# Masking the local attention's probabilities on GpSimd in place of band products on TensorE, with five probability slots and small weight steps

## The reference

```python
i = jnp.arange(x.shape[1])
diff = i[:, None] - i[None, :]
mask = (diff >= 0) & (diff < WIN)          # local attention, WIN = 32; the global one has diff >= 0 alone
scores = jnp.einsum('bhqd,bhkd->bhqk', q, k) / np.sqrt(HD).astype(np.float32)
scores = jnp.where(mask, scores, jnp.float32(-1e+30))
probs = jax.nn.softmax(scores, axis=-1)    # 16 heads of 8, 4 key heads
...
x = x + global_latent_attn(rmsnorm(x, norm1_w), ...)
x = x + local_gqa_attn(rmsnorm(x, norm2_w), ...)
...
w_q = jnp.clip(jnp.round(W / scale), -1.0, 1.0) * scale     # feed-forward weights, scale = mean |W| of a row
```

## Time and profile before

| what | us |
|---|---|
| median of three runs (lowest, highest) | 529.55 (525.73, 531.33) |
| the profiled execution, its own time | 528.51 |
| its span, from the first to the last instruction | 526.7 |
| PE, DVE, ACT, POOL busy in the span | 435.2, 345.2, 342.2, 197.6 |
| granted TensorE clock, mean of the span (1.00 is 2.4 GHz) | 0.946 |

### The profile page before, as it was taken

One profiled execution on the slowest core, in us unless ns is written; L12 is line 12 of the kernel. 1 busy time (PEld: TensorE's weight loads), 2 busy tenths in 40 slices (PEclk: granted clock), 3 DMA queues, 4 the chain that ended last, 5 costly groups with the idle time before them and its releaser, 6 DMA issues.

```text
span 526.7 us, 15578 instructions
## 1 busy us (share of the span) xinstructions
PE 435.2 (83%) x6044; PEld 226.5 (43%) x6044; DVE 345.2 (66%) x940; ACT 342.2 (65%) x442; POOL 197.6 (38%) x482
## 2 busy tenths in 40 slices
PE   0245899998999999889999998999999998657362
PEld 0122444453464445544564454445545544414231
DVE  2899986755377758858668573655782476664556
ACT  0143689889767889758787983999878975104010
POOL 4458667878334253715311250131330011051101
PEclk9999799999899999999999998999999999679577
DMA  7311421112201010110100011000020000010000
GB/s 198 117 40 42 86 47 42 41 43 46 39 2 41 12 43 3 43 41 12 43 3 1 11 39 5 11 4 2 2 49 7 1 7 7 0 40 13 1 1 10
DMA packets 47528, 15.77 MB, mean 30 GB/s; under 512 B 40536, under 2 KB 46816, under 8 KB 47456
## 3 DMA queue, kind: packets, MB, share of 16 engines
q1 hardware_dynamic: 44032, 12.10, 10.7%
q10 hardware_dynamic: 3424, 2.68, 1.8%
HBM read 4.15 MB, written 1.05 MB: 10 GB/s over the span
## 4 chain that ended last, share of the span: by engine, by line
PE 54%; DVE 20%; POOL 8%; issue 6%; DMA 4%; ACT 4%; SPq 3%; DVEq 0%; POOLq 0%; ACTq 0%
PE osum_g L995 17%; PE scores L966 13%; PE scores L960 4%; PE misc L1094 4%; PE misc L1105 4%; PE misc L995 3%; ACT prob L840 3%; DMA qT<-qe_l 3%; PE misc L1031 2%; DVE early L1419 2%; PE misc L936 1%; DVE early L1221 1%; SPq L686 1%; PE misc L1012 1%; SPq L672 1%
## 5 line engine op out<-in xcount | busy, mean ns | idle before, releaser
L840 ACT ACTIVATE prob<-scores 128x1024 f32<-128x1024 f32 (+3 forms) x352 | 308.0, 930 | 107.0 <-PE scores L966 105.4
L995 PE MATMUL osum_g<-prob,V 128*32 128x256 f32 (+1 forms) x2304 | 150.6, 385 | 2.7 <-POOL prob L782 2.7
L966 PE MATMUL scores<-qT,kT 32*128 32x256 f16 (+2 forms) x1520 | 113.4, 257 | 13.8 <-ACT prob L840 10.4
L995 PEld LDWEIGHTS osum_g<-prob,V 128*32 128x32 f32 x2304 | 63.4, 112 | 56.7 <-issue 30.0
L966 PEld LDWEIGHTS scores<-qT,kT 32*128 32x128 f16 x1520 | 38.9, 92 | 95.8 <-issue 87.4
L782 POOL TENSOR_SCALAR_AFFINE_SELECT prob<-prob 128x512 f32<-128x512 f32 x64 | 42.8, 685 | 79.7 <-ACT prob L840 79.0
L1105 PE MATMUL misc<-t2T,h1p 128*128 128x512 f16 x128 | 34.6, 419 | 13.3 <-DVE h1p L1451 9.7
L1458 DVE TENSOR_TENSOR early<-misc,oh 128x512 f32<-128x512 f32 x32 | 21.9, 684 | 24.0 <-PE misc L1105 22.8
L799 POOL TENSOR_SCALAR frs<-fmv 128x1 f32<-128x1 f32 x16 | 3.1, 196 | 91.0 <-DVE fmv L1474 90.9
L1094 PE MATMUL misc<-early,t1T 128*128 128x256 f16 x256 | 34.0, 293 | 1.5 <-DVEq L1422 1.5
L960 PE MATMUL scores<-band,identb 128*32 128x320 bf16 (+1 forms) x512 | 27.9, 303 | 7.6 <-DMA qT<-qe_l 7.1
(11 more groups left out here) (213 smaller groups left out, 637.9 us busy)
## 6 DMA issues: line engine op xcount, KB each, us to landing
X<-in_L_attn_hidden_dram SPq DMA_DIRECT2D x8, 128.0 KB, 4.8
early<-in_L_ffn_expert_w_dram ACTq DMA_DIRECT2D x1, 1024.0 KB, 7.9
out_dram<-X SPq DMA_DIRECT2D x16, 64.0 KB, 1.5
rope<-in_rope_dram SPq DMA_DIRECT2D x1, 256.0 KB, 3.8
early<-in_L_ffn_shared_w_dram ACTq DMA_DIRECT2D x2, 128.0 KB, 9.0
qT<-qe_l SPq DMA_TRANSPOSE x16, 2.4
kT<-ke_g SPq DMA_TRANSPOSE x8, 2.8
qT<-qe_g SPq DMA_TRANSPOSE x8, 2.7
```

The source lines that it names most:

```text
L840: act.activation(prob[:, n % NP, 2 * half:2 * half + 2, lo:hi], src, ACT.Exp, scale=float(HD) ** -0.5 * QSCALE ** -2).then_inc(exp_done, 1)
L966: ins = pe.matmul(scores[:, 512 * m + c:512 * m + c + w], kT[a][rows, t % kept[a], g, :], query_rows(a, b, g, rows, q, w), start=(a == G a ...
L995: ins = pe.matmul(o[32 * m:32 * m + 32, at + q:at + q + w], V[a][:, t % kept[a], V_AT[g]:V_AT[g] + 32], prob[:, n % NP, m, c:c + w], start ...
```

## The change

For the local units of blocks 0 to 6 PE no longer writes the band; the scores are computed for all of the 320 columns (288 in block 0), the exponential is taken of all of them, and POOL multiplies the probabilities by a table `keep` of ones and zeros, one `tensor_tensor` for each half, in `qkmask`. Block 7 keeps its band (`BANDED = 7`). The table `keep` (128x320 fp32) is one more DMA on ACT's queue, and all waits for that group of DMAs count 15 in place of 14. `prob` has five slots in place of four. `prep` is cut into eight steps and `ternary` into eighteen, and the planner's durations, its delay for DMAs and the table `PULL` are others, so that the order on every engine is another. A step "fill" is in the planner but off (`FILL = 0.0`).

```diff
-NP = 4
+NP = 5
...
-HOP = (0.22, 0.1, 0.08, 0.2, 2.5)
+HOP = (0.22, 0.1, 0.08, 0.2, 2.6)
...
-    "unitg": (749.2, 939.7, 409.5, 154.3, 1050, 121.7, 460.4, 510.3),
+    "unitg": (591.3, 418.6, 393.1, 426.3, 686.7, 411.3, 365.5, 623.9),
...
-        op((DVE, "prep"), 6.8, (DVE, "weights"), earliest=LANDED)
+        for k, t in enumerate((0.35, *[0.95] * 6, 1.8)):
+            op((DVE, "prep", k), t, (DVE, "prep", k - 1) if k else (DVE, "weights"), earliest=LANDED)
...
-        for k, t in enumerate((3.9, 3.9, 2.0, 2.85, 2.85)):
-            op((DVE, "ternary", k), t, (DVE, "prep"), *([(DVE, "ternary", k - 1)] if k else []))
+        for k in range(2 * (NE + 1)):
+            op((DVE, "ternary", k), 1.05 if k <= NE else 0.8, (DVE, "ternary", k - 1) if k else (DVE, "prep", 7))
...
-        op((SP, "qT", a, b), 0.5, (DVE, "split", a, b), *([("Q", a, o, *units_of(a, o)[-1])] if o >= 0 else []))
+        op((SP, "qT", a, b), 1.2 if g else 2.4, (DVE, "split", a, b), *([("Q", a, o, *units_of(a, o)[-1])] if o >= 0 else []))
...
+            kept = diag or not g and b < BANDED
...
-            if diag:
-                op(("M", *u), 1.34, ("E", *u))
+            if kept:
+                op(("M", *u), 1.34 if g else 3.0, ("E", *u))
...
             def qkmask(*u):
                 n = UNIT[u]
+                lo, hi = columns(*u[:2], u[3])
+                if u[0] == L:
+                    pool.wait_ge(wf_in, 16 * 15)
                 for half in range(2):
                     pool.wait_ge(exp_done, 2 * n + half + 1)
+                    if u[0] == L:
+                        d = prob[:, n % NP, 2 * half:2 * half + 2, lo:hi]
+                        k = keep[:, lo:hi].unsqueeze(1).broadcast_to([P, 2, hi - lo])
+                        pool.tensor_tensor(d, d, k, ALU.mult).then_inc(mask_done, 1)
+                        continue
...
+                act.dma_start(keep[:], keep_d).then_inc(wf_in, 16)
...
-                if a == L:
+                banded = a == L and b >= BANDED
+                if banded:
                     lo, hi = columns(a, b, pr)
...
-                                        kT[a][rows, t % kept[a], g, :], query_rows(a, b, g, rows, q, w), start=(a == G and k == 0), stop=True,
+                                        kT[a][rows, t % kept[a], g, :], query_rows(a, b, g, rows, q, w), start=(not banded and k == 0), stop=True,
...
+    keep = (band == 0).astype(np.float32)
```

More of the change, by code:

```diff
@@ L142, in front @@
         op((ACT_E, "xT", a, b), 0.37, (PE, "xT", a, b), *old(DVE, "proj", a, p))
-        op((PE, "proj", a, b), 0.83, (ACT_E, "xT", a, b), *([] if b else [(DVE, "weights") if g else (DVE, "prep")]),
+        op((PE, "proj", a, b), 0.83, (ACT_E, "xT", a, b), *([] if b else [(DVE, "weights") if g else (DVE, "prep", 0)]),
            bank=[((DVE, "proj", a, b), -1.5)])
@@ L149, in front @@
         op((DVE, "split", a, b), 2.99, (POOL, "proj", a, b), *old(SP, "qT", a, p))
-        op((SP, "kT", a, b), 0.5, (POOL, "ksplit", a, b), *([("Q", L, p, KVH - 1, 0)] if b > 1 and not g else []))
+        op((SP, "kT", a, b), 1.2, (POOL, "ksplit", a, b), *([("Q", L, p, KVH - 1, 0)] if b > 1 and not g else []))
         o = b - Q_KEPT[a]
-        op((SP, "qT", a, b), 0.5, (DVE, "split", a, b), *([("Q", a, o, *units_of(a, o)[-1])] if o >= 0 else []))
+        op((SP, "qT", a, b), 1.2 if g else 2.4, (DVE, "split", a, b), *([("Q", a, o, *units_of(a, o)[-1])] if o >= 0 else []))
     def attend(self, a, b):
@@ L198, in feed @@
             op((PE, "fmask", b, i), 0.62, (PE, "fmask", b, 0) if i else (PE, "fohT", b), bank=[((DVE, "fmask", b, i), 0)])
-            op((DVE, "fmask", b, i), 1.32, (PE, "fmask", b, i), (DVE, "fmask", b, 0) if i else (DVE, "fohT", b), (DVE, "ternary", 4))
+            op((DVE, "fmask", b, i), 1.32, (PE, "fmask", b, i), (DVE, "fmask", b, 0) if i else (DVE, "fohT", b), (DVE, "ternary", 2 * NE + 1))
         op((PE, "fw1s", b), 0.95, (DVE, "fohT", b), (PE, "fmask", b, 1), (SP, "wturn", 0), (SP, "wturn", 1),
@@ L373, in make_plan @@
         t, e, k = best
+        late = not queues[G] and not current and not exps
+        while FILL and late and t > free[PE] + FILL / clock.rate + 0.02 and free[PE] > max(half):
+            order[PE].append(("fill", len(units)))
+            free[PE] = clock.run(free[PE], FILL)
         if k[0] == "qk" and e == PE:
@@ L458, in build @@
         band = sb("band", [P, 2 * P + 2 * WIN], BF16)
+        keep = sb("keep", [P, 2 * P + 2 * WIN])
         rank = sb("rank", [P, NE])
@@ L1150, in weights, with prep, limits @@
                 dve.tensor_copy(rwT[:], bank(s, 2)[:, 0:NE]).then_inc(free(s, 2), 1)
[L1152 to L1157 removed]
+            def prep(k):
+                if k == 0:
+                    dve.wait_ge(wf_in, 16 * 15)
+                    dve.tensor_scalar(wqkv[L][:], wraw[L][:], nw[L][:, 0:1], None, ALU.mult).then_inc(wqkv_ready, 1)
+                elif k < 4:
+                    r = slice((k - 1) * (NE + 1) * FT // 3, k * (NE + 1) * FT // 3)
+                    dve.tensor_reduce(s1c[:, r], w1n[:, r, :], AX.X, ALU.add, apply_absolute_value=True)
+                elif k < 7:
+                    r = slice((k - 4) * (NE + 1) // 3, (k - 3) * (NE + 1) // 3)
+                    link(dve.tensor_reduce(s2c[:, r], w2n[:, r, :], AX.X, ALU.add, apply_absolute_value=True))
+                else:
+                    limits()
+            def limits():
                 link(dve.tensor_scalar(s1c[:], s1c[:], 1.0 / P, 1e-5, ALU.mult, ALU.max))
@@ L1217, in ternary @@
                 ter2, low2 = [t.rearrange("p (k d) -> p k d", d=FT * P) for t in (t2, t2b)]
-                rows = sorted({(w, r) for w, r, _ in TURNS[k]})
+                rows = [(1, 2 * k), (1, 2 * k + 1)] if k <= NE else [(2, k - NE - 1)]
                 for w, r in rows:
```

58 lines of the change are left out of this document (26 added, 32 removed).

## The result

The changed kernel takes 558.55 us (median of 4 runs, 558.37 to 560.23) beside 529.64 us of the kernel before (4 runs, 525.73 to 531.33). The ratio is 1.0564, with a 95% interval from 1.0503 to 1.0626. The forecast was 513.0 us, with 498 to 530 as its range: it is wrong in sign.

What follows compares the result with a forecast made beforehand. It took PE to bound the middle stretch (100 to 441 us), DVE the start, and a chain over all engines the end. 528.5 - 20.7 - 3.5 + 5.0 + 3.7 = 513.0 us, range 498 to 530.

Steps and rivals of the forecast that it cites:

- band products removed: PE, local units of blocks 0 to 6: dropping the band products wins 20.7 us, bounds 14.3 and 24.7.
- start, order: Start of the run: earlier key split and q transpose, no wait for `bdiag`; wins 3.5 us, bounds 0 and 9.
- masks on POOL: PE waits for POOL's masks before local products with V: costs 5.0 us, bounds 0 and 29.
- DVE held up: Middle stretch: POOL's multiplications lock DVE out of shared ports; costs 3.7 us, bounds 0 and 22.
- so I let a sixth through: 3.7 us: Middle stretch: of 22 us lost on DVE, a sixth reaches the run time, 3.7 us.
- half of its work as of the kind that is stopped: Middle stretch: DVE busy 0.64, half its work stoppable, so 0.32 of 69 us is lost: 22 us.
- DVE has 124 us free there: Middle stretch, 100 to 441 us: DVE is idle 124 us, a reason for letting little lost time through.
- The sign that it named for this: Sign of the locks: PE waits for DVE's `hm` and `h1p` of over 10 us would show the forecast wrong.
- 220 us free in the middle: Middle stretch: POOL, busy 121 of 341 us, has 220 us free for 81 us of multiplications.
- first rival: Blocks 0 and 1: POOL becomes the bound early and no gain comes before 147 us; 525.4 us, chance 0.14.
- slower rival: Feed-forward and fronts, 100 to 420 us: DVE becomes what PE waits for; 538.8 us at half, chance 0.10.
- second rival: The slower one: DVE, losing 69 us to locks, becomes what PE waits for; 538.8 us at half, chance 0.10.

Runs made afterwards that it cites:

- no mask: Changed kernel with neither band products nor POOL multiplications, so the local mask of blocks 0 to 6 is left out: 515.40 us, 0.9756 against before.
- order with band: Changed kernel's order, tables and five slots, with band products back in blocks 0 to 6 and no POOL multiplication: 531.70 us, 1.0069 against before.
- awaited writes: Changed kernel with two POOL writes of zeros to an unread tile replacing each multiplication, PE waiting for them as for masks: 531.33 us.
- idle writes: Changed kernel with two POOL writes of zeros to an unread tile replacing each multiplication, PE not waiting for them: 535.20 us.
- idle multiplication: Changed kernel with each POOL multiplication done on a tile nobody reads, so PE waits for no mask: 555.27 us, 1.0503 against before.

## Why the prediction was wrong, point by point

| term of the sum | predicted, us | measured, us | from |
|---|---|---|---|
| band products removed | -20.7 | -16.5 | no mask, less order with band |
| start, order | -3.5 | +3.6 | order with band |
| masks on POOL | +5.0 | +16.4 | awaited writes, less no mask |
| DVE held up | +3.7 | +26.3 | changed kernel, less awaited writes |
| sum | -15.5 | +29.8 | |

How the last two rows share their 42.7 us hangs on the kernels compared: by the versions for which PE does not wait it is 21.2 (idle writes, less no mask) and 18.3 (idle multiplication, less idle writes). By either way both terms were far too small. The band's 16.5 us lie inside the bounds that the prediction gave, 14.3 and 24.7.

The failing step is "so I let a sixth through: 3.7 us". The mechanism was named, and its upper bound on DVE, 69 us, was sound: 45.0 us were lost (392.7 - 347.7). Both factors after it were too small. The first, DVE's busy share times "half of its work as of the kind that is stopped", took 0.32 of the 56 holds and gave 22 us. In the trace 44 instructions were held beside 56 multiplications, 0.79, for 1.06 us each where the row had 1.24. An instruction that is stopped waits whatever its size, so counting busy time misses that small instructions in chains lose as much as large ones: `lrk` has 16 columns and lost 1.3 us. And "DVE has 124 us free there" is true of the mean and says nothing of a chain for whose end PE waits: in both chains shown above five instructions are held nearly in a row. Of the 45.0 us, 26.3 reached the end, more than half (18.3 by the other comparison), where the prediction let a sixth through. The sign that it named for this came at other places: PE's waits for `h1p` in the middle are 3.6 us, but for PSUM banks, `oh`, `xn` and `fh` they are the rest of 28.6.

The second step that failed is the price of POOL's time. The prediction set 81 us against "220 us free in the middle" and charged only the waits for the masks. These were small, as it said: 2.2 us for 5.0. The multiplications are 89.9 us for 81 (1.61 us for 1.45 each; at 640 columns from 1.52 to 2.01). But in most blocks they stand in pieces of 11 to 14 us, and other steps wait behind a piece: the prediction named the key split and the next diagonal mask and put no price on them, and in the kernels with writes it is above all `frs`. That is the mechanism of the first rival, POOL as the bound; only it is not early. Between the changed kernel and no mask, the last global product of blocks 2, 4, 6 and 7 comes 1.6, 18, 38 and 41 us later (taken at ACT's copy behind it): the loss grows from block to block, and not at the start.

The slower rival had the place, the price (69 us on DVE) and the point of decision (a third, 24.2 us). 26.3 of 69 is just past that point, so by the rival's own prices DVE alone would have made the kernel about equal. It became 5.6% slower because what the two rivals price, weighed as alternatives, was paid in one kernel.

The start won less than its rows promised: `split` began at 25.68 for 28.40 and the wait for `bdiag` is gone, but the first scores came at 32.31 for 32.95, not at 31.5. The transpose of k was issued at 28.08, not at 27.32 as before, and that of q behind it at 29.46 for 30.17: 0.7 of the 1.5 us. PE's waits for the transposed q went down too, from 6.4 to 0.5 us. None of it is seen in the time of the order with band, which is 3.6 us longer than before; which part of the order costs this stays open.

Two readings were off without weight. The 448 band products in the earlier trace rows are those of blocks 1 to 7; blocks 0 to 6 hold 384 of them and 64 of 288 columns, about 24.4 us in all. And block 1's last local unit begins its band at 148.00 us, so these units do not end at 147.

The lower clock is a part of these terms, not one more. No mask and the changed kernel have the same 5596 instructions on PE; their busy time is 415.1 us at a mean clock of 0.932 and 430.3 at 0.895. So 15.2 of the 41.6 us between their spans are PE at work more slowly, and 26.4 are PE idle. The awaited writes, at 426.7 us and 0.906 in a span of 530.8, tell which term brings which: from no mask to these, 11.6 of 15.7 us are slower work; from these to the changed kernel only 3.6 of 25.9, and 22.3 are PE idle. So POOL's time was paid mostly at a lower clock, and DVE's holds mostly as waits. The prediction priced waits by their length alone.

On the rule that it weighed, the Trainium skill, "SBUF — State Buffer", section "SBUF: two separate sides": DVE instructions with two SBUF inputs and GpSimd instructions that read SBUF exclude each other on a shared pair of ports for whole instructions; a GpSimd instruction that only writes does not hold them up. By that rule the trace agrees: under the writes, which read nothing, two-input `acc` stays at 292 ns, and beside the multiplication it takes 521. Taken at one for one, as the prediction read it, 90 us would have been put on DVE; 45 came, as not every multiplication meets a DVE instruction that can be held. That tells nothing of what reaches PE.

## What to carry to other kernels

Work moved to an engine "with time to spare" was paid at three places here: what stands behind it in that engine's order, who shares a port with it, and the clock of the engine that waits in the end (PE's mean fell from 0.932 to 0.895). Before pricing GpSimd work with two SBUF inputs, list the DVE chains that run beside it and count their all-SBUF instructions: each can lose about one GpSimd instruction (1.06 us of 1.61 here), however small it is. Price the second engine's load by a dummy of the same length that nobody needs: two such kernels, one that reads and one that only writes, told the two costs apart here, though not exactly, as they do not simply add.

## What the runs showed of the hardware that was not expected

A DVE instruction with one operand in PSUM is not held at all: the four of L1481 that ran beside a multiplication in the changed kernel took 691 ns, as they do with no mask. Nor were two `BATCH_NORM_STATS2` of `fo` (294 ns) and one reduction of an SBUF tensor (`ss_l`, 486 ns). The prediction had this as an argument against its second rival, without a count. The cast of `h1p`, with one SBUF input, is held by POOL's writes too, though less: beside writes three of four took 0.81 to 1.08 us, for 0.43 alone and 1.64 to 1.66 beside the multiplication. Of the tensor-scalar instructions some are: three of four `xn_g` took 0.69 to 0.88 us for 0.34, while three `fl` beside writes kept their 0.35.

A multiplication by a table on POOL takes at least 1.40 us for 576 columns, 1.52 for 640, 0.48 for 144, 0.51 for 160 and 0.35 for 80; cutting the 56 of them in four costs POOL 26 us (115.6 for 89.9).
